# Attention with relative positions: three score banks, band exp at its copy, shift rows by block transpose

## The reference, cut to what matters

```python
idx = jnp.clip(r[None, :] - r[:, None], -M, M) + M          # M = 128, r = arange(2048)
content = jnp.einsum('bhqd,bhkd->bhqk', q, k)
relative = jnp.einsum('bhqd,qkd->bhqk', q, rel_k[idx])
w = jax.nn.softmax((content + relative) / jnp.sqrt(jnp.float32(hd)), axis=-1)
out = jnp.einsum('bhqk,bhkd->bhqd', w, v) + jnp.einsum('bhqk,qkd->bhqd', w, rel_v[idx])
x = x + (out @ Wo.T + bo) * silu(ffn(xn))
```

## Time and profile before

| | before |
|---|---|
| median of 3 runs | 2638.44 us (2637.92 to 2640.88) |
| profiled execution, its own time | 2641.73 us |
| its span, first to last instruction | 2640.0 us |
| mean granted TensorE clock | 0.973 of full speed |
| scores (L957) run from, to | 179.9 to 2203.3 us |
| probabilities (L966) run from, to | 248.9 to 2259.4 us |

### The profile page before, as it was taken

The page is one execution under the profiler, slowest core; times in us unless marked ns, Lnnn a source line. Parts: engine busy times, 40 slices in busy tenths (PEclk is TensorE's granted clock), DMA queues, the critical chain, the costliest instruction groups (busy, mean ns, idle before and its releaser), DMA issues. The chain is left out here.

```text
span 2640.0 us, 47807 instructions
## 1 busy us (share of the span) xinstructions
PE 2420.9 (92%) x15216; PEld 1184.1 (45%) x15216; DVE 1828.1 (69%) x4985; ACT 1749.4 (66%) x4026; POOL 884.5 (34%) x1977
## 2 busy tenths in 40 slices
PE   6838999999999999999999999999999999799998
PEld 3412444444444444444444444444444444567666
DVE  6558777777777777777777777777777774233333
ACT  4514877777777777777777777777777777321121
POOL 1222454333333333333333333333333332133332
PEclk9955999999999999999999999999999999999999
DMA  5668889777777777777777777777777762642221
GB/s 160 176 141 265 244 268 243 235 222 230 233 230 237 225 222 233 234 231 236 232 228 234 231 236 236 231 226 226 233 231 238 227 194 88 244 144 69 66 64 53
DMA packets 351151, 541.00 MB, mean 205 GB/s; under 512 B 30608, under 2 KB 259392, under 8 KB 350912
## 3 DMA queue, kind: packets, MB, share of 16 engines
q1 hardware_dynamic: 336880, 502.76, 61.8%
q0 software_dynamic: 14032, 35.24, 4.5%
HBM read 272.60 MB, written 269.43 MB: 205 GB/s over the span
## 5 line engine op out<-in xcount | busy, mean ns | idle before, releaser
L1073 DVE TENSOR_REDUCE part<-ps 128x1 f32<-128x512 f32 (+3 forms) x2048 | 1189.5, 591 | 457.8 <-PE ps L957 438.8
L1135 ACT ACTIVATE probs_T<-pst 128x512 f32<-128x512 f32 (+3 forms) x2048 | 985.3, 525 | 397.4 <-PE pst L966 390.0
L957 PE MATMUL ps<-k_front,q_front 96*128 96x512 bf16 x2048 | 790.1, 393 | 13.0 <-DVE part L1071 2.5
L915 PE MATMUL pout<-probs_T,v_far 128*32 128x512 f32 (+3 forms) x4864 | 550.8, 533 | 40.4 <-ACT probs_T L1111 31.4
L822 POOL TENSOR_TENSOR left_T<-probs_T,left_mask 128x128 f32<-128x128 f32 x512 | 219.5, 429 | 991.7 <-ACT probs_T L1111 797.4
L957 PEld LDWEIGHTS ps<-k_front,q_front 96*128 96x128 bf16 x2048 | 198.6, 97 | 587.8 <-DVE part L1073 296.8
L966 PE MATMUL pst<-q_back,k_left 102*128 102x512 bf16 (+3 forms) x1024 | 349.7, 343 | 0.7 <-ACT probs_T L1135 0.6
L966 PE MATMUL pst<-q_back,k_right 102*128 102x512 bf16 (+3 forms) x1024 | 348.8, 342 | 0.5
L1148 ACT ACTIVATE band<-band,negm 128x384 f32<-128x384 f32 (+1 forms) x512 | 305.5, 597 | 0.1
L1071 DVE CUSTOM_DVE_ANT_0 band<-ps,band 128x256 f32<-128x256 f32 (+2 forms) x704 | 300.5, 427 | 0.0
L915 PEld LDWEIGHTS pout<-probs_T,v_far 128*32 128x32 f32 x4864 | 174.5, 108 | 237.9 <-issue 211.4
(11 more groups left out here) (160 smaller groups left out, 2112.0 us busy)
## 6 DMA issues: line engine op xcount, KB each, us to landing
rel_scores<-rel SPq DMA_DIRECT2D x128, 1024.0 KB, 7.9
band_probs<-band SPq DMA_DIRECT2D x128, 768.0 KB, 3.9
pwin<-band_probs SPq DMA_DIRECT2D x128, 512.0 KB
band<-rel_scores SPq DMA_DIRECT2D x64, 768.0 KB
band<-rel_scores SPq DMA_DIRECT2D x64, 576.0 KB, 5.2
w<-in_w_dram SPq DMA_DIRECT2D x16, 1024.0 KB, 14.3
band<-rel_scores SPq DMA_DIRECT2D x64, 128.0 KB, 5.7
q_terms<-terms SPq DMA_DIRECT2D x48, 128.0 KB
```

Source lines behind the costliest of these rows:

```text
L915: return nc.tensor.matmul(pout[32 * g:32 * g + 32, c0:c1], values, probs, start=first, stop=False, skip_group_check=True)
L957: nc.tensor.matmul(ps1[u % 2][:, :], q_front[a.par][:, a.s * P:(a.s + 1) * P], k_front[a.par][:, u * CW:(u + 1) * CW], start=True, stop=Tr ...
L1073: ins = nc.vector.tensor_reduce(peak, src, AX_X, ALU.max)
L1135: ins = nc.scalar.activation(probs_T[t.s % 2][:, u * CW + c0:u * CW + c1], pst[u % 2][:, c0:c1], ACT.Exp, scale=SCALE)
```

## The change

PSUM is dealt out anew: `ps1` gets a third bank, and `psmall` is gone. The two strip blocks share `pband` with two of the band blocks; the third band block lies in the last quarter of `prel`, beside the relative scores. Score banks are counted through by `score_slot`, since the turn-back now takes a turn in the same three banks (`turned_slot`) and no longer uses `prel`; its step is one later.

The exp of the band leaves its own pass. GpSimd subtracts the row maximum from the band in place in every step (off - 4); `negm` is gone. The strip in DRAM and the band blocks then hold scores, and ScalarE takes their exp while it copies them out of PSUM: `near_keys` in the same step as the transposes, in two pieces since the third block lies in another bank, and `window`, which moves from VectorE to ScalarE. TensorE's transposes (`turn_band_and_window`) move from the end of the step into u2, behind the far scores of u2 and ahead of the scores of u3. They wait for `winT_evac`, `bandT_evac` and `r_evac`, and `near_keys` waits for both sets; the relative scores wait for `bandT_evac`.

The shift rows no longer pass through TensorE. `shb` has 32 places a step, VectorE transposes it in blocks of 32x32 into `shT` (at the end of the step with off one above a multiple of 4), and GpSimd copies the rows under `q_back` in four copies of six partitions, at the beginning of the following step, each waiting for the one before.

```diff
LOWEST = -3.0e38
+NO_KEY = -1.0e9
...
 LAG_T = 18
-LAG_O = LAG_T + 5
+LAG_O = LAG_T + 6
...
-        shb = two("shb", [P, CH, SHIFTS], BF16)
+        shb = two("shb", [P, CH, 32], BF16)
+        shT = sb("shT", [P, CH, 32], BF16)
...
-        ps1 = [ctx.enter_context(nc.psum_tensor(f"ps1_{i}", [P, 512], F32)) for i in range(2)]
+        ps1 = [ctx.enter_context(nc.psum_tensor(f"ps1_{i}", [P, 512], F32)) for i in range(3)]
...
-        psmall = ctx.enter_context(nc.psum_tensor("psmall", [P, 512], F32))
-        pnear = psmall[:, 0:NEARW]
-        prow = psmall[0:SHIFTS, NEARW:512].bitcast(BF16)
+        pnear = pband[:, 2 * P:4 * P]
+        pthird = prel[:, 3 * P:4 * P]
...
+        def score_slot(hb, off, u):
+            step = hb * 2 * NB + off
+            return CH * step + u + turned_before(step, u)
+        def turned_slot(hb, off):
+            step = hb * 2 * NB + off
+            return min(CH * step + 3, CH * NB * NBH) + turned_before(step, 2)
...
+                    pool.memset(shb[p][:, :, :], 0.0).then_inc(const_set, 1)
...
+                    pool.memset(band[p][:, 0, 0:P], NO_KEY).then_inc(const_set, 1)
+                    pool.memset(band[p][:, NB - 1, BAND - P:BAND], NO_KEY).then_inc(const_set, 1)
...
                 def step(hb, off):
+                    q = Step(hb, off - 6)
+                    if off % CH == 2 and q.valid:
+                        pool.wait_ge(rows_tp, q.count(4, q.r + 1))
...
+                        left = Step(hb, off - LAG_T - 2)
+                        if left.valid:
+                            pool.wait_ge(left_ready, left.count(16, left.s + 1))
+                        sides = Step(hb, off + LAG_R - 4)
+                        pool.wait_ge(sides_done, sides.count(4, sides.r + 1) if sides.valid else NBH * 4)
+                        lower = Step(hb, off - 5)
+                        pool.wait_ge(band_ready, lower.count(16, lower.s + 1) if lower.valid else NBH * 16)
+                        if off % NB == 10:
+                            pool.wait_ge(v_built, q.count(1, 1))
+                        if hb == 0:
+                            pool.wait_ge(slots_set, 16)
+                        if hb in (1, 2):
+                            pool.wait_ge(slots_filled, 16 * (TILES if hb == 2 else min(off, TILES)))
+                        rows = q_back[q.par][ROWS:ALLROWS, q.r * CW:(q.r + 1) * CW].rearrange("p (g b c) -> p b g c", g=CH, b=P // 32)
+                        for b in range(P // 32):
+                            if b > 0:
+                                pool.wait_ge(rows_link, q.count(12, 3 * q.r + b))
+                            ins = nc.gpsimd.tensor_copy(rows[:, b], shT[32 * b:32 * b + SHIFTS, :, :])
+                            ins.then_inc(rows_link if b < P // 32 - 1 else rows_copied, 1)
+                        pool.wait_ge(rows_copied, q.count(4, q.r + 1))
 
...
-                        wait(pool, band_ready, y.count(16, 4 * y.r + 4 - 32))
-                        nc.gpsimd.tensor_tensor(negm[y.par][:, four], rmax[y.par][:, four], neg_scale[:, 0:1].to_broadcast([P, CH]),
-                                                ALU.mult).then_inc(negm_ready, 1)
+                    if y.valid:
+                        if y.g > 0:
+                            pool.wait_ge(rmax_ready, y.count(4, y.r + 1))
+                        bl = band_blocks(y.s)
+                        s = band[y.par][:, y.s, (bl[0] - y.s + 1) * P:(bl[-1] - y.s + 2) * P]
+                        nc.gpsimd.tensor_scalar(s, s, rmax[y.par][:, y.s:y.s + 1], None, ALU.subtract).then_inc(band_ready, 1)
...
-                    def shift_rows():
-                        pe.wait_ge(shift_ready, y.count(4, y.r + 1))
-                        wait(pe, rows_copied, y.count(4, y.r))
-                        if w.valid:
-                            wait(pe, winT_evac, w.count(16, w.s + 1))
-                        for g in range(CH):
-                            mm = nc.tensor.transpose(prow[0:SHIFTS, g * P:(g + 1) * P], shb[y.r % 2][:, g, :], con["ident_bf"][:, :])
-                        mm.then_inc(rows_tp, 1)
                     def turn_back():
+                        bank = turned_slot(hb, off)
                         pe.wait_ge(out_evac, o.count(1, 1))
-                        wait(pe, norm_done, o.count(1, 0))
-                        wait(pe, r_evac, x.count(16, x.s + 1) if x.valid else NBH * 16)
+                        wait(pe, s1_used, bank - 2)
                         for r in range(CH):
-                            mm = nc.tensor.transpose(prel[:, r * P:(r + 1) * P], pwin_T[:, 0, S - CW + r * P:S - CW + (r + 1) * P], con["ident"][:, :])
+                            mm = nc.tensor.transpose(ps1[bank % 3][:, r * P:(r + 1) * P], pwin_T[:, 0, S - CW + r * P:S - CW + (r + 1) * P], con["ident"][:, :])
                         mm.then_inc(back_mm, 1)
...
+                    def turn_band_and_window():
+                        bl = band_blocks(t.s)
+                        pe.wait_ge(band_ready, t.count(16, bl[-1] + 1))
+                        wait(pe, bandT_evac, t.count(16, t.s))
+                        wait(pe, winT_evac, t.count(16, t.s))
+                        if bl[-1] > t.s:
+                            pe.wait_ge(r_evac, x.count(16, x.s + 1) if x.valid else NBH * 16)
+                        for i in bl:
+                            b = t.s - i + 1
+                            mm = nc.tensor.transpose(pthird if i > t.s else pband[:, (i - t.s + 1) * P:(i - t.s + 2) * P], band[t.par][:, i, b * P:(b + 1) * P], con["ident"][:, :])
+                        mm.then_inc(bandT_mm, 1)
+                        if t.g == 0:
+                            pe.wait_ge(win_in[t.r % 2], t.count(32, 16 * (t.r // 2 + 1)))
+                        for b in range(2):
+                            mm = nc.tensor.transpose(pnear[:, b * P:(b + 1) * P], pwin[t.r % 2][:, t.g, b * P:(b + 1) * P], con["ident"][:, :])
+                        mm.then_inc(winT_mm, 1)
...
-                            wait(pe, s1_used, a.count(64, 4 * a.s + u - 1))
-                            nc.tensor.matmul(ps1[u % 2][:, :], q_front[a.par][:, a.s * P:(a.s + 1) * P], k_front[a.par][:, u * CW:(u + 1) * CW],
+                            wait(pe, s1_used, score_slot(hb, off, u) - 2)
+                            nc.tensor.matmul(ps1[score_slot(hb, off, u) % 3][:, :], q_front[a.par][:, a.s * P:(a.s + 1) * P], k_front[a.par][:, u * CW:(u + 1) * CW],
...
                             wait(pe, r_evac, x.count(16, x.s))
-                            if t.s == LAG_O - LAG_T:
-                                wait(pe, norm_done, t.count(1, 0))
+                            last = Step(hb, off - LAG_T - 1)
+                            if last.valid:
+                                pe.wait_ge(bandT_evac, last.count(16, last.s + 1))
                             nc.tensor.matmul(prel[:, 0:RELS], q_front[x.par][:, x.s * P:(x.s + 1) * P], con["rel_k"][:, :], start=True, stop=True).then_inc(r_mm, 1)
-                        if u == 1 and off % CH == 2 and y.valid:
-                            shift_rows()
                         if u == (2 if w.s == 0 else 1) and w.valid:
                             key_values()
                         if u >= 2 and w.s == NB - 1 and w.valid:
                             pe.wait_ge(winT_evac, w.count(16, 16))
                             near_values(u - 2).then_inc(near_pv, 1)
+                        if u == 2 and t.valid:
...
+                        wait(dve, shift_ready, last.count(4, last.r + 1 - 8))
+                        wait(dve, band_ready, last.count(16, 4 * last.r + 4 - 32))
...
+                    def shift_rows():
+                        dve.wait_ge(shift_ready, shifted.count(4, shifted.r + 1))
+                        wait(dve, rows_copied, shifted.count(4, shifted.r))
+                        nc.vector.transpose(shT[:, :, :].rearrange("p g k -> p (g k)"), shb[shifted.r % 2][:, :, :].rearrange("p g k -> p (g k)")).then_inc(rows_tp, 1)
+                    def normalise():
+                        back = ps1[turned_slot(hb, off) % 3][:, :].rearrange("p (r g d) -> p r g d", r=CH, g=CH)
+                        rv = rden[:, :].rearrange("p (r g) -> p r g", r=CH)
+                        dve.wait_ge(back_mm, o.count(1, 1))
+                        if o.n > 0:
+                            dve.wait_ge(s1_used, turned_slot(hb, off - NB) + 1)
+                        nc.vector.reciprocal(rv, back[:, :, :, HD]).then_inc(den_ready, 1)
+                        dve.wait_ge(den_ready, o.count(1, 1))
+                        dst = attn[:, o.n, :, :].rearrange("p (g r) d -> p r g d", g=CH)
+                        nc.vector.tensor_tensor(dst, back[:, :, :, 0:HD], rv.unsqueeze(3).to_broadcast([P, CH, CH, HD]), ALU.mult).then_inc(s1_used, 1)
 
...
-                        if u == 0 and w.valid:
-                            window()
...
+                        if u == CH - 1 and off % CH == 1 and shifted.valid:
```

(40 more changed lines are left out.)

65 lines of the change are left out of this document (13 added, 52 removed).

## The result

| | before | after |
|---|---|---|
| median of four runs | 2639.43 us (2637.92 to 2640.88) | 2738.86 us (2735.72 to 2740.22) |
| profiled execution, and its span | 2641.73, 2640.0 | 2737.59, 2735.7 |
| mean granted clock | 0.973 | 0.959 |

The change makes the kernel slower: after over before is 1.0378, with a 95% interval of 1.0365 to 1.0391. The forecast was 2581 us, and the range ended at 2665.

A forecast was written before the change was run, and what follows sets the result against it. TensorE was taken as the bound: 63.4 us a round, 56.9 of it floor. With exp waits 3.1, GpSimd lateness 0.95 and other waits 0.5 it becomes 61.4; 31 rounds save 62, last steps add 5: 2581 us, range 2515 to 2665.

The forecast's parts named there:

- The DMAs and SyncE's order are the same: DMA engines and SyncE: nothing changes, and engines 74% busy stay below their limit; no cost was booked.
- c: Price of GpSimd's added 384-column subtraction in each step: taken as 0.65 us, from slopes giving 0.46 and 1.0.
- the second rival: GpSimd's in-order queue makes the left block's mask late for ScalarE: 4.0 us a round, 2677 us; chance 0.17.
- m: Price of each of GpSimd's four shift-row copies in every fourth step: taken as 0.4 us, between 0.28 and 0.51.
- the exp wait: TensorE's u1 probability matmul waits for the exp of u3: 0.20 us in most steps, 3.1 a round.
- both slow rivals: GpSimd late, 2677 us, chance 0.17; ScalarE's chain of copies and exps longer than a step, 2680 us, chance 0.08.
- The forecast's own case: A round falls from 63.4 to 61.4 us, giving 2581 us; chance 0.56 for a round of 60 to 63.
- The term of 2.9 for the shift rows: TensorE no longer turns shift rows: 0.73 us in each of four steps, 2.9 us a round gone.
- The ring through ScalarE: Band transposes need ScalarE's relative-score copy: 3.34 us against a 3.5 step, not binding; as rival 2680 us, chance 0.08.
- The last rival: On TensorE an exp wait only replaces the score-bank wait, GpSimd half late: 63.4 us a round, 2640 us; chance 0.05.
- All three signs of being wrong: Subtraction over 0.9 us, exp u0 waiting for left_T in every fourth step, or band transposes waiting for the relative copy.
- GpSimd 65 to 75% busy: GpSimd's busy share after the change, listed among the signs of being right; it was 34% before.

The follow-up runs named there:

- experiment 1: The changed kernel with its 32 token-slot scatters spread, one in every fourth step over rounds 2 to 9: 2658.4 us.
- experiment 10: The kernel before with only GpSimd's wait for the slot scatters' landing added, in every fourth step of rounds 2 to 5: 2692.0 us.
- experiment 8: experiment 1 with GpSimd's subtraction written as two tensors, the maximum broadcast, instead of a tensor and a scalar pointer: 2593.2 us.
- experiment 2: experiment 1 with the subtraction of the row maximum moved from GpSimd to VectorE: 2570.2 us.
- experiment 9: The kernel before with only the shift rows taken off TensorE, transposed and copied by VectorE; two score banks and the old order stay: 2627.8 us.
- experiment 4: experiment 1 with two score banks instead of three: 2707.8 us.
- experiment 11: experiment 5 with two score banks instead of three: 2553.2 us.
- experiment 5: experiment 2 with the transposes and the band exp back at the end of the step, behind u3: 2515.0 us.
- experiment 7: The changed kernel with the subtraction and row copies on VectorE, scatters left in rounds 2 and 3, no landing wait on GpSimd: 2598.5 us.

## Why the prediction was wrong, step by step

**The step that failed first is "The DMAs and SyncE's order are the same".** The DMAs are the same, but a wait for one was added on GpSimd, and my sum has no term for it: it counts four copies and nothing ahead of them. The scatter's row of 1.06 is not its landing. The trace before gives no landing time for these scatters, as nothing waits for them one by one there, so the term could only have been left open, with a chance of its own; it was put at nothing. It cost 80 us in the changed kernel (experiment 1) and 53 in the kernel before (experiment 10). One difference of the two is in the traces: in the changed kernel TensorE also waits for the row copies behind the landing, twice, 20.6 in all, and in experiment 10 the rows don't pass through GpSimd. That this makes up most of the 27 isn't shown by a run.

**The size that failed is c.** The text had a subtraction at 0.65 between 0.46 and 1.0, and put the turning point at 0.9; it measured 1.24. I had taken the nearest row "of the same kind" (one input, 128 columns), a select, with no scalar read through a pointer; the same form at 384 and 256 columns gives (1243 - 923)/128, 2.5 ns a column, against 2.1 by the two-input slope that made my upper bound. The upper end of an unseen operation should not have been the nearest slope. By the page that I cited (the Trainium skill's GPSIMD Engine Reference, "Elementwise — side-by-side cycle accounting"), 2.6 cycles an element come to 0.83 for the two-input form before dispatch, an estimate. The trace agrees at this size, with 0.827 for the whole row in experiment 8; at 1016 columns the page's figure would give 2.20, and the row has 1.88, so "the two-input rows agree" said too much. The form with a pointer costs half as much again.

**The mechanism of the second rival was right.** Put c = 1.24 and m = 0.35 into its own count: the mask is done at 1.5 + 1.24 + 0.45 + 1.24 + 2.0 + 1.4 + 0.1 + 0.45 = 8.38, 0.73 late. Less 0.25 of slack this is 0.48 three times, and 0.73 + 1.4 - 0.25 = 1.88 once: 3.3 a round. Set step against step, the kernel after is behind experiment 2, where GpSimd has no subtraction, by 1.79 behind v_far, by 0.58 and 0.43 in two other places and by nothing in the fourth: 2.8 a round. Experiment 8 is a second trial of the count: c = 0.83 makes only the step behind v_far late, by 1.06, and it is 0.94 late there. The whole round comes to 56.9 + 3.1 + 3.3 + 0.5 = 63.8, and measured 63.9, but that agreement is in part luck: the exp wait was 0.4 dearer than 3.1, and GpSimd's lateness 0.5 cheaper than 3.3. My range, too, ended at 2665, under both slow rivals' own figures (2677 and 2680), though I gave these a chance of 0.25 together.

**The forecast's own case was right once both were out.** Experiment 2 has a round of 61.0 and 2570 us, against 61.4 and 2581. The exp wait is 0.26 in place of 0.20 and 3.5 a round in place of 3.1, so the count from start to start had the right place and was 0.4 a round short; ScalarE's band exp starts 0.37 behind the start of the last transpose (1010.24 to 1010.61 in experiment 2), where I had 0.31. Experiment 2 has one more VectorE operation than the forecast (0.45 a step) and GpSimd's lateness isn't in it, so the near agreement of the two totals is in part luck.

**The term of 2.9 for the shift rows was mis-sized as a term.** Alone it is 0.6 a round (experiment 9), since other waits, for VectorE's reduces and for ScalarE's band copy, grow into the room. The third bank is worth 1.2 to 1.6 (experiments 4 and 11). Gains on an engine that also waits don't add up one by one.

**The ring through ScalarE** doesn't bind by itself: in the changed kernel the band transposes wait for the relative copy (25.6 us in 20 rounds), but in experiment 2, where GpSimd isn't late, that wait is gone. What I didn't price is the same bank the other way round, the relative scores waiting for the third band block's exp: next to nothing with the transposes ahead of u3, 2.0 a round with them at the end (experiment 5). The last rival, a score bank's wait replaced by an exp's, is true of the third bank in part (experiment 4). All three signs of being wrong showed: a subtraction over 0.9, the mask holding up ScalarE (twice a round, not in every fourth step) and transposes waiting for the relative copy; turn-backs are 63.9 apart, not 61.4. "GpSimd 65 to 75% busy" held (69%), and told nothing: it would have held in the slow case too.

Accounting in medians: 2739 after; less 80 for the landing wait; less 88 for GpSimd's subtraction, 2570; less 55 for the transposes moved ahead of u3, 2515. With these three choices replaced the rest of the change is worth 124 us against the kernel before. The third bank is 38 of them (experiment 11); how the others divide between the moved band exp and the shift rows wasn't taken apart.

## What to carry to other kernels

Go through each wait that a change adds, ask which event raises its semaphore, and price a DMA's landing from issue to landing, with all that is queued behind the waiting instruction; a wait that lasts for two rounds of 32 can outweigh a gain in all of them. Price an operation that the trace doesn't show by its exact form, operand kinds included, and let the upper bound lie well above the nearest slope when an in-order queue has only a few tenths of slack. When an engine is freed, look at whether its neighbours' waits fill the room, before the full time is booked as a gain. And when two tiles share a bank, price both directions: each must find the other's copied out.

## What the runs showed of the hardware

- On GpSimd a subtraction of 384 columns by a scalar pointer took 1.24 us, the same with the scalar broadcast as a second tensor 0.83, and on VectorE 0.45.
- VectorE's block transpose of the shift rows (128x128 bf16) took 0.30 us in the kernel after, within the bound of 0.42 that the prediction gave it; each copy of six rows took 0.29 on GpSimd and 0.23 on VectorE.
- An indirect scatter shown for 1.06 us landed 2.3 to 9.1 us after its issue, 5.9 in the median; in experiment 7, where nothing waits for it, 4.2 to 11.4, 7.6 in the median.
- TensorE's granted clock fell where the engine had stood still: in rounds 2 and 3 of the kernel after it went between the 2.4 and the 1.2 GHz level, with a mean of 0.81, while TensorE waited up to 10.8 us at a time, and in experiment 10 the mean was 0.86; in the steady stretch it was 1.00. Behind the 10.8 us wait a score matmul took 0.61 us, against 0.38 just ahead of it. The lower clock made some 19 of the 84 us in the one and 20 of the 55 in the other.
